# A three-block perceiver layer on one core: first batch's gate, mixing, norm and network products moved forward among the state pairs, second norm's statistics taken from the first's

## What is computed

```python
x = x + xattn(layernorm(x), ctx)                 # network: relu(out @ W1 + b1) @ W2 + b2
u = layernorm(x)                                 # outer norm, no gain or shift
h = layernorm(u) * ln1_g + ln1_b                 # "second norm" of the title: a norm of a norm
r = rmsnorm(h) * rms_w
xi, z = split(r @ in_proj)                       # 512 and 512 columns
xc = silu(conv4(xi) + conv_b)
dt, B, C = split(xc @ x_proj)                    # 64, 16 and 16 columns
delta = softplus(dt @ dt_proj + dt_b)
for each token:  s = exp(delta * A) * s + delta * xc * B ;  y = sum_n(s * C)     # 16 states per channel
h = h + ((y + Dp * xc) * silu(z)) @ out_proj
v = u + h
v = v + relu(layernorm2(v) @ ffn_w1 + b1) @ ffn_w2 + b2                          # 512-2048-512
x = x + v
x = x + quantised_network(layernorm(x))
```

## Time and profile before

| | |
|---|---|
| median of 3 runs | 3171.7 us (3169.69 to 3173.9) |
| the profiled execution | 3170.58 us, its span 3168.5 us |
| busy: PE, PE weight loads, DVE, ACT, POOL | 3045.8, 1833.7, 2268.5, 1697.6, 1930.1 us |
| the chain that ended last, by engine | PE 82%, DVE 14%, issue 1%, ACT 1%, POOL 1% |
| mean granted TensorE clock | 0.984 |

### The profile page before, as it was taken

How to read it: one execution, slowest core, us unless ns; L and a number is a source line. 1 busy time by engine, 2 the same in 40 slices (tenths; PEclk the granted TensorE clock), 3 DMA queues, 4 the chain that set the end, 5 groups by cost and what they waited for, 6 DMA issues and landing times.

```text
span 3168.5 us, 41413 instructions
## 1 busy us (share of the span) xinstructions
PE 3045.8 (96%) x15408; PEld 1833.7 (58%) x15408; DVE 2268.5 (72%) x3635; ACT 1697.6 (54%) x2967; POOL 1930.1 (61%) x487
## 2 busy tenths in 40 slices
PE   7999999999999999999999999999999877899999
PEld 4666666666666666666666666666534332344477
DVE  7777777777777777777777777777747799995653
ACT  2566666666666666666666666666641455330021
POOL 1688888988888888988888888888850000000000
PEclk9999999999999999999999999999999888899999
DMA  5422222222223233232223222232131112124100
GB/s 151 127 51 71 72 75 61 61 74 72 71 51 79 68 94 91 61 83 64 71 51 87 60 71 61 71 82 55 46 141 38 41 66 94 53 80 160 67 14 17
DMA packets 100683, 230.13 MB, mean 73 GB/s; under 512 B 22850, under 2 KB 27970, under 8 KB 99234
## 3 DMA queue, kind: packets, MB, share of 16 engines
q1 hardware_dynamic: 100484, 227.49, 26.3%
HBM read 114.46 MB, written 8.06 MB: 39 GB/s over the span
## 4 chain that ended last, share of the span: by engine, by line
PE 82%; DVE 14%; issue 1%; ACT 1%; POOL 1%; DMA 0%; SPq 0%; ACTq 0%; DVEq 0%; POOLq 0%
PE ps L1777 15%; PE ps L1738 15%; PE ps L1764 12%; PE ps L1691 9%; PE ps L1722 9%; DVE pm L997 7%; PE ps L1715 6%; PE ps L1978 4%; PE ps L1942 3%; PE ps L1789 3%; PE ps L1958 2%; DVE bx L1238 1%; PE ps L1750 1%; PE ps L1746 1%; POOL psum L854 1%
## 5 line engine op out<-in xcount | busy, mean ns | idle before, releaser
L997 DVE TENSOR_REDUCE pm<-ps 128x1 f32<-128x512 f32 x2048 | 1406.4, 691 | 623.6 <-PE ps L1738 549.2
L1462 ACT ACTIVATE pf<-ps 128x512 f32<-128x512 f32 x2048 | 1217.3, 601 | 776.7 <-PE ps L1764 700.7
L854 POOL TENSOR_TENSOR psum<-psum,pf 128x2048 f32<-128x2048 f32 x254 | 1167.1, 4595 | 139.2 <-ACT pf L1462 127.8
L1738 PE MATMUL ps<-ks,qs 96*128 96x512 f32 x2048 | 854.2, 417 | 26.9 <-DVE pm L997 24.7
L1764 PE MATMUL ps<-qs,ks 98*128 98x512 f32 x2048 | 814.3, 399 | 2.1 <-ACT pf L1462 1.9
L854 POOL TENSOR_TENSOR psum<-pf 128x2048 f32<-128x2048 f32 x127 | 581.4, 4578 | 183.0 <-ACT pf L1462 183.0
L1738 PEld LDWEIGHTS ps<-ks,qs 96*128 96x128 f32 x2048 | 387.0, 189 | 319.5 <-issue 213.2
L1777 PE MATMUL ps<-pf,V 128*32 128x512 f32 x4096 | 493.9, 600 | 0.0
L1764 PEld LDWEIGHTS ps<-qs,ks 98*128 98x128 f32 x2048 | 390.7, 191 | 49.6 <-ACT pf L1462 11.3
L863 POOL PARTITION_ALL_REDUCE qstat<-qstat x2 | 0.7, 366 | 630.3 <-DVE qstat L1274 630.3
L1715 PE MATMUL ps<-cTh,Wkg 128*128 128x512 f32 x732 | 292.7, 400 | 3.0 <-ACT V L1451 0.4
(11 more groups left out here) (214 smaller groups left out, 3100.8 us busy)
## 6 DMA issues: line engine op xcount, KB each, us to landing
ks<-KH SPq DMA_DIRECT2D x512, 128.0 KB, 2.4
ks<-KL SPq DMA_DIRECT2D x256, 128.0 KB, 2.4
cT<-in_ctxT SPq DMA_DIRECT2D x32, 768.0 KB, 4.6
Wkg<-wk_rows SPq DMA_DIRECT2D x61, 384.0 KB, 3.0
BC<-bc_rows SPq DMA_DIRECT2D x32, 512.0 KB, 4.8
ring<-in_ffn_w SPq DMA_DIRECT2D x16, 1024.0 KB, 5.4
wA<-in_W_fcT SPq DMA_DIRECT2D x4, 1024.0 KB, 10.1
wB<-in_W_projT SPq DMA_DIRECT2D x4, 1024.0 KB, 7.0
```

The source lines that it names most:

```text
L854: pool.tensor_tensor(acc, before, pf[:, tile % P_SLOTS, :], ALU.add).then_inc(s_sum, 1)
L997: dve.tensor_reduce(pm[:, n // BLK, n % BLK:n % BLK + 1], src, AX.X, ALU.max).then_inc(s_wfree, 1)
L1462: act.activation(pf[:, tile % P_SLOTS, j * NTOK:(j + 1) * NTOK], ps[:, S_BANK + u % S_BANKS, :], ACT.Exp, scale=SCALE).then_inc(s_exp, 1)
L1738: last = pe.matmul(dst, qs[0:3 * HD, h, t * P:(t + 1) * P], ks[0:3 * HD, keys_of(of, j), i * 512:(i + 1) * 512], start=True, stop=True)
```

## The change

It edits the schedule's constants, the list of units, the norm of a norm, batch 0's step sizes, and adds one small activation:

```diff
-DELTA_1 = DT_1 + 4
-GATE_0 = S_ALL - 2
-MIX_0 = S_ALL + 2
+DELTA_1 = S_ALL - 2
+GATE_0 = {S_ALL - 1: (0, 1, 2), S_ALL: (3,)}
+GATE_1 = PAIRS - 2
+MIX_0 = S_ALL
 LN2_0 = MIX_0 + 1
 TURN_2 = LN2_0 + NT // 2
-FFN1_0 = TURN_2 + 2
+FFN1_0 = TURN_2 + 1
 FFN2_0 = FFN1_0 + F2 // P
 MIX_AT = PAIRS - FFN2_0 + 2
-AHEAD_1 = 5
+AHEAD_1 = 4
...
-     + stage(1, "xw1")[:AHEAD_1] + stage(0, "rms_T") + stage(0, "xz")[:6] + stage(0, "dbc") + stage(0, "xz")[6:7]
-     + stage(0, "dt") + stage(0, "xz")[7:] + stage(1, "xw1")[AHEAD_1:]),
+     + stage(1, "xw1")[:AHEAD_1] + stage(0, "rms_T") + stage(0, "xz")[:6] + stage(0, "dbc") + stage(0, "dt")
+     + stage(0, "xz")[6:] + stage(1, "xw1")[AHEAD_1:]),
...
+        above = place("above", 120 * K, [P, KD, NTOK])
...
+            def spread_of_normal(b, t):
+
+                root = std[b][:, t:t + 1]
+                dve.tensor_scalar(msq[b][:, t:t + 1], mv[b][:, t, 1:2], root, root, ALU.mult, ALU.mult
+                                  ).then_inc(s_var[b], 1)
+                roots[b] += 1
+                return roots[b]
+
+            def scaled_normal(b, t, n):
+
+                root = std[b][:, t:t + 1]
+                dve.wait_ge(s_std[b], n)
+                link(dve.reciprocal(root, root))
+                link(dve.scalar_tensor_tensor(hr[b][:, t, :], xa[b][:, t, :], root, m1b[:, 1, :], ALU.mult, ALU.mult))
+                link(dve.tensor_tensor(hr[b][:, t, :], hr[b][:, t, :], m1b[:, 2, :], ALU.add))
...
-                        normalise(b, k - 1, var_of[b, k - 1, "xa"], xa[b], hr[b], m1b[:, 1, :], m1b[:, 2, :])
+                        scaled_normal(b, k - 1, var_of[b, k - 1, "xa"])
...
-                        var_of[b, k, "xa"] = spread_of(b, k, xa[b])
+                        var_of[b, k, "xa"] = spread_of_normal(b, k)
...
+            def positive_part(e):
+
+                w = (0, "dt", e)
+                dve.wait_ge(s_abs, e + 1)
+                empties(dve.tensor_scalar(above[:, e, :], bank(w), col("dt_b", e), 0.0, ALU.add, ALU.max), w)
+
+            def step_sizes_0(e):
+
+                if e == 0:
+                    unit_ready(dve, (0, "xz", 2 * KD - 1))
+                    convolved(dve, 0)
+                dve.wait_ge(s_ln, e + 1)
+                link(dve.tensor_tensor(delta[0][:, e, :], above[:, e, :], dx[0][:, e, :], ALU.add))
+                dve.tensor_tensor(dx[0][:, e, :], delta[0][:, e, :], xc[0][:, e, :], ALU.mult
+                                  ).then_inc(s_delta, 1)
...
+                for e in GATE_0.get(j, ()):
+                    gate(0, e)
                 if DELTA_1 <= j < DELTA_1 + KD:
                     step_sizes(1, j - DELTA_1)
-                if GATE_0 <= j < GATE_0 + KD:
-                    gate(0, j - GATE_0)
...
             for e in range(KD):
-                step_sizes(0, e)
+                positive_part(e)
+            for e in range(KD):
+                step_sizes_0(e)
...
             def decays(b):
 
+                if b == 0:
+                    act.activation(warm[:], col("eps"), ACT.Exp)
...
             dbc_of(0)
+            dt_of(0)
             xz(0, 6)
-            dt_of(0)
             xz(0, 7)
```

More of the change, by code:

```diff
@@ L374, in emit @@
         qmax = sb("qmax", [P, Q_PARTS])
+        warm = sb("warm", [P, 1])
         COL = {}
@@ L1212, in beside @@
                     second_norm(0, 3)
-                if GATE_0 + S_ALL <= j:
-                    gate(1, j - GATE_0 - S_ALL)
+                if GATE_1 <= j:
+                    gate(1, j - GATE_1)
             attended(1)
```

## The result

The changed kernel took 3146.71 us (median of 4 runs, 3143.74 to 3147.78) against 3172.49 (4 runs) for the kernel before: ratio 0.9918, 95% interval 0.9901 to 0.9936, so between 20 and 31 us faster. The forecast was 3151.0, range 3146.5 to 3157.0. On the 3171.7 us of the forecast's base the ratio gives 3145.7, just under the range. Ratios here are of fast runs alone; one run of the kernel before, beside the first experiments, took 10792.6 us in the slow state and counts in none of them.

The account below looks back on a forecast made before the run. DVE was taken to bound the kernel up to up(0, 0), PE from there. The terms 3.2 + 5.9 + 11.6 = 20.7 us took the profiled 3170.6 to 3149.9, or 3151.0 for a median; range 3146.5 to 3157.

Parts of the forecast that it names:

- Part 1: Ahead of the pairs: four step sizes take 5.3 us instead of 8.46, gain 3.2 us.
- I take no gain: First y_sum ahead of the pairs: idle PE before it falls from 6.89 to about 2.9 us, costed at no gain.
- Part 2: Batch 1's norms, pairs 2 to 9, DVE full: four tiles save 1.47 us each, 5.9 us.
- the small instruction behind them only changes its operands: Norm tile: dropping statistics and aggregation saves 0.94 us, with the small instruction behind them costed as unchanged.
- Part 3: Pairs 28 to 36: up(0, 0) 16.7 us earlier, three more y_sums (5.15) behind it, gain 11.6 us.
- the wait of 1.4 at pair 30: Pair 30: DVE waits for the decays, which ACT begins behind its logarithms and a table load; forecast 1.5 us.
- y_sum(36) takes 3.4, as y_sum(38) did behind 2.6 us of idle time: Just ahead of up(0, 0): y_sum(36) at half clock, 3.4 us; at full clock the gain is 11.6 + 1.5.
- rival E: More gain: both half-clock y_sums run at full speed, 3147.5 us; chance 0.1.
- Part 4: From up(0, 0) and the tail: PE full to down 15, two downs just cover DVE; costed at nothing, 0.5 at worst.
- B: Mixing at half clock behind y_sum(32): DVE waits 12.6 us in all, 3163.6 us; chance of all or part 0.13.
- C: Norm stretch paced by PE's xw2 products or ACT, 1.5 us stall each pair in 28 to 32: 3165 to 3171; chance 0.05.
- D: TensorE, cold at pair 36, stays at half clock: 5.15 us more each pair, 3192 at 8 pairs; chance 0.03.

Follow-up runs that it names:

- e2_lead: Kernel before with only the edits ahead of the pairs (AHEAD_1 = 4, dt products ahead of xz 6, positive parts, early Exp table load): 3173.62 us, ratio 1.0001.
- e1_norm: Kernel before with only the cheaper norm, in both batches: 3166.09 us against 3172.97, ratio 0.9981.
- e3_sched: Kernel before with only the moved pairs (step sizes at 30, gates at 31 and 32, mix at 32, network products from 36): 3158.81 us, ratio 0.9952.
- e5: Changed kernel, unchanged, run again for a second trace and more times: 3147.36 us against 3171.3, ratio 0.9925.
- e6: Changed kernel with xz(0, 6) put back ahead of the dt products: 3148.26 us.
- e7: Changed kernel with the network's start, FFN1_0, one pair later (up(0, 0) at 37): 3154.53 us.
- e9: Changed kernel with ACT's silus of xz 6 and xz 7 moved behind its logarithms, ahead of the first decays: 3144.49 us.
- e8: Changed kernel with batch 1's logarithms on ACT moved from pair 26 to 28: 3146.92 us.
- e11: Changed kernel with silus behind logarithms, batch 1's first norm a pair later, its logarithms at pair 28, its first B and C loaded before the weight pieces: 3142.16 us, ratio 0.9907.
- e10: Changed kernel with silus of xz 6 and 7 behind the logarithms, and batch 1's norms and logarithms one pair later: 3147.52 us against 3171.3, ratio 0.9924.
- e4: Kernel before, unchanged, run again for a second trace: 3172.51 us for its one execution.
- e12: Kernel before with only the cheaper norm, run once more for one trace: 3165.03 us.

## Why the prediction was right, and where it was wrong

**Part 1, 3.2 us: right, link by link.** xz(0, 0) came 3.44 earlier. The silu of xz 6 stood at 2461.39, on the clock of the trace before (2.69 later) 2464.08; forecast 2464.0. The first logarithm was there for DVE's first step size at 2469.96, on that clock 2472.65; forecast about 2472.5. First `inputs` 3.23 earlier. That its gain rests on the cheaper norm was said ("in time"), and `e2_lead` shows it: alone it gives nothing. The term "I take no gain" for the first y_sum was 0.6 too low: it took 2.72 instead of 3.75, and DVE's wait at the first norm fell from 2.29 to 1.70.

**Part 2, 5.9 us: 5.40.** In the changed kernel and in `e1_norm` alike. The passes saved what was costed (0.52 of 0.53 a tile). The statistics were costed at 0.94; "the small instruction behind them only changes its operands" was the slip: L1090 takes 0.27 instead of 0.15 and holds the next instruction back by 0.11 more, so 0.83 is left. 4 x (0.52 + 0.83) = 5.4. Had the dropped pass cost the 0.33 us that I estimated from the Trainium skill (VectorE: DVE Perf Modes, the errata-adjusted cycle table), the stretch would have given some 4.5; the trace agrees with the row (0.55), not with the estimate.

**Part 3, 11.6 us: 11.64 alone, 13.09 in the whole.** The nine pairs, the step sizes and gates, the wait of 1.4 at pair 30, no wait at `mixed`: all there. **The step that failed is the size of one term: "y_sum(36) takes 3.4, as y_sum(38) did behind 2.6 us of idle time".** It took 1.98, worth 1.45. That y_sum at full clock is half of what rival E named; I gave E 0.1, and placed the lower end of the range by its price, with both y_sums at full clock. In `e3_sched`, where y_sum(36) took 3.43, Part 3 came out as summed. In nine traces of eight kernels with the moved schedule, y_sum(36) ran at full clock in five (`e5` to `e7`, `e9` and the changed kernel) and at or near half clock in four (`e3`, `e8`, `e11`; 2.91 in `e10`), which is nearer to even chances than to 0.1.

**Part 4, nothing: right.** PE has no gap from `up(0, 0)` to down 15, and the transposes follow the two downs at once.

**Rivals.** B (mixing at half clock), C (pace set elsewhere) and D (cold through the dense stretch) did not come: clock 1.00 from 2707.48 on, and no wait at `mixed`. A small form of B did come elsewhere: the first pair of mix products took 7.97 and 7.74 in the two traces of the norm alone and 7.42 to 8.18 in `e3`, `e8`, `e10` and `e11`, instead of 7.03.

**The sum.** By the traces 3.23 + 0.59 + 5.40 + 13.09 = 22.3 us behind the attention, against 20.7: 1.6 us short, 1.4 of it y_sum(36), 0.6 the first y_sum, less 0.5 for the norms. On the base of 3171.7 that is 3149.4, inside the range.

The runs gained more than that. All 36 runs of the kernel before that the ratios count, from four sets, have a mean of 3172.2, the 8 of the changed kernel one of 3146.9: 25.3 apart, give or take about 1.5 (my estimate from their spread), where both pairs of traces have 22.3 behind the attention. The forecast had 20.7, so by these means the miss is 4.6 us, and the step that failed is 1.4 of it. Some 3 us of the measured gain stand in no term, and on the base of the forecast these took it past the range. Their cause stays open. In the traces they lie in the attention stage, which ended 2.7 us earlier in the first pair and 2.4 in the second. But it ended anywhere from 2354.80 to 2359.37 in 14 traces with no edit to it, and on average only 0.7 earlier in the 8 traces of the changed kernel and its variants (mean 2357.0) than in the 6 of the kernel before and its variants (2357.7). Behind the attention the traced executions need not be typical either: those of the norm alone lay 2.2 us apart. The range had no term for such differences; its low end was the price of E, less 1.

**What stays open** is what sets the clock at these short gaps. The idle time just ahead does not: y_sum(36) ran at full clock behind 3.03 us and at half behind 2.44, and in the changed kernel's trace another y_sum took 3.25 behind 3.16 us (at 2655.89), a third 1.98 behind 2.52 (at 2535.13). What goes with it in all traces is the stretch one y_sum earlier. A line groups traces; it gives the y_sum ahead of the transposes with the idle time before it, the transposes, and the next y_sum (38 in the last line but for e10, else 36):

| kernel | idle before, us | transposes, us | next y_sum, us |
|---|---|---|---|
| after; e5; e6; e7; e9 | 9.49; 9.57; 9.45; 9.44; 9.67 | 2.04; 1.96; 2.08; 2.09; 1.91 | 1.98 in all five |
| e3; e8; e11 | 9.02; 8.88; 8.87 | 2.50; 2.64; 2.65 | 3.43; 3.57; 3.58 |
| before; e4; e1; e12; e2; e10 | 8.32 in five; 8.40 | 2.52; 2.52; 3.10; 2.99; 2.46; 3.18 | 3.42; 3.41; 3.12; 3.35; 3.78; 2.91 |

Where PE had stood for 9.4 us and more and the transposes ran at full clock almost from their start, the next y_sum did too. It is a coincidence seen in 14 traces, not a mechanism shown. No run changed that idle time alone. The chip alone does not decide it: `e5` to `e7` and `e10` ran on one chip, `e8`, `e9` and `e11` on another, and each of the two has both outcomes.

## What to carry to other kernels

Cost a moved schedule by the engine that is full in each stretch, and count the parts behind a mark that the change leaves alone; here the sum then held to 1.6 us behind the attention, and missed the measured times by some 4. Time saved on an engine is kept only as far as the next resource that ends last: here four buffers that PE empties, a load behind four weight pieces in one queue, or TensorE's clock after a short gap each took 1 to 3.4 us of it. Where matmul groups stand behind gaps of 1 to 3 us, put both clock levels for each of them into the range, and beside them how far the stages that nobody touched differ from trace to trace (here 4.6 us).

## What the runs showed of the hardware that I had not expected

The clock at a short gap was fixed neither by the length of the gap nor by the program. Two traces of the kernel before agreed within 0.02 us behind the attention, two of the changed kernel within 0.04, with the attention ending 1.9 and 2.1 us later; I took that for a rule. The Trainium skill (TensorE: Matmul & The Clock Gate, Part 1) says that the place where a cold engine speeds up varies from run to run of one kernel. The two traces of the norm alone agree with it, though they come from two chips: y_sum(39) 3.47 and 1.98, the mix products 7.97 and 7.74, the end 808.71 and 806.52.

Four kernels show a gain of DVE's taken back by this clock: `e8_logs_later` (1.4 us gained, 1.6 lost at y_sum(36)), `e1_norm`, and in a smaller measure `e6_xz6_first` and `e9_silu_behind_logs`, in whose traces the y_sum ahead of batch 1's in_proj took 3.78.

Tiny vector instructions differ in price: the `tensor_scalar` on 128x1 with two per-partition scalars took 0.27 us and held the next one back 0.19, the one with constants took 0.15 and held it back 0.08, four times in the pairs. Reading a fresh result does not explain it: the old one (L903) reads `mv`, which the instruction just before wrote, while L1090's root was written before a 0.55 us pass.
